# A new step list for a one-core transformer layer, 64x64 tiles for the W1 products, and MLP weights transposed on the host

## What is computed

```python
# attention part: 4 heads of 64 with fast weights W0, W1, W2; 4 chunks of 128 tokens
def step(carry, xi):
    W0, W1, W2, M0, M1, M2 = carry
    out = einsum(silu(qi @ W0.T) * (qi @ W2.T), W1)
    dhidden = einsum('bco,boh->bch', vi, W1)
    ...
    dw0 = dw0 + M0 * mm                      # and dw1, dw2
    dw0 = _newtonschulz5(dw0)                # five iterations: A = X X^T, B = bA + cAA, X = aX + BX
    return renorm(W0 + dw0, n0), ...
# beside it: windowed softmax attention with 2 heads of 128; both sums go through Wo
x = x + _layernorm(attention(_layernorm(x)))
# MLP
h = gelu(xn @ proj1.T + proj1_bias)          # proj1 (1024, 256)
out = h @ proj2.T + proj2_bias               # proj2 (256, 1024)
x = x + _layernorm(out)
```

## Time and profile before

| | |
|---|---|
| median of 3 runs | 419.19 us |
| profiled execution | 418.44 us |
| its span, first to last instruction | 416.7 us |
| mean granted TensorE clock | 0.994 |
| PE busy | 387.9 us (93%) |
| PEld busy | 310.6 us (75%) |
| DVE busy | 273.9 us (66%) |
| ACT busy | 225.7 us (54%) |
| POOL busy | 195.3 us (47%) |
| HBM traffic | 24 GB/s |

### The profile page before, as it was taken

One profiled execution on the slowest core, in us unless ns is written; L12 is line 12 of the kernel. 1 busy time (PEld: TensorE's weight loads), 2 busy tenths in 40 slices (PEclk: granted clock), 3 DMA queues, 4 the chain that ended last, 5 costly groups with the idle time before them and its releaser, 6 DMA issues.

```text
span 416.7 us, 15706 instructions
## 1 busy us (share of the span) xinstructions
PE 387.9 (93%) x6574; PEld 310.6 (75%) x6574; DVE 273.9 (66%) x720; ACT 225.7 (54%) x444; POOL 195.3 (47%) x273
## 2 busy tenths in 40 slices
PE   5998997999999999988999999997989999998994
PEld 5477856887668887877667888776788757886883
DVE  3359998788245869897545883888657582587113
ACT  1599654556852378635994632562445674444510
POOL 4366673557551534675250592643235070367114
PEclk9899999999999999999999999999999999999999
DMA  6830100000000000022000000000300000010001
GB/s 155 294 95 5 49 2 2 5 4 5 2 2 4 13 3 2 2 77 70 3 2 6 5 0 2 2 2 4 104 5 3 5 2 2 1 52 0 2 1 50
DMA packets 12293, 10.83 MB, mean 26 GB/s; under 512 B 4160, under 2 KB 11712, under 8 KB 12224
## 3 DMA queue, kind: packets, MB, share of 16 engines
q1 hardware_dynamic: 12224, 9.83, 7.7%
HBM read 7.73 MB, written 2.10 MB: 24 GB/s over the span
## 4 chain that ended last, share of the span: by engine, by line
PE 64%; DVE 10%; issue 5%; POOL 5%; ACT 1%; POOLq 0%; DVEq 0%; ACTq 0%
PE pair L782 14%; PE pair L791 9%; PE pair L684 6%; PE pair L672 6%; PE pair L697 5%; PE pair L661 4%; PE pair L750 3%; PE pair L566 3%; POOL fro L1389 2%; PE pair L717 2%; PE pair L538 2%; PE pair L623 1%; PE pair L609 1%; POOL u_n L1389 1%; PE pair L547 1%
## 5 line engine op out<-in xcount | busy, mean ns | idle before, releaser
L782 PE MATMUL pair<-xn2T,p1T 128*128 128x512 f32 (+1 forms) x160 | 58.1, 511 | 0.6 <-ACT xn2T L815 0.6
L791 PE MATMUL pair<-p2T,h 128*128 128x256 f32 x256 | 56.7, 381 | 0.0
L1394 POOL TENSOR_SCALAR var<-mv 128x1 f32<-128x1 f32 (+1 forms) x52 | 12.3, 236 | 90.5 <-DVE mv L1358 56.5
L791 PEld LDWEIGHTS pair<-p2T,h 128*128 128x128 f32 x256 | 48.2, 190 | 6.4
L782 PEld LDWEIGHTS pair<-xn2T,p1T 128*128 128x128 f32 x160 | 29.4, 190 | 19.5 <-issue 17.5
L1059 DVE SCALAR_TENSOR_TENSOR A<-pair,eye 128x512 f32<-128x512 f32 x45 | 28.6, 683 | 15.4 <-PE pair L672 15.2
L822 ACT ACT_TABLE_LOAD x28 | 35.9, 1283 | 2.1 <-PEq L1535 1.7
L1059 DVE SCALAR_TENSOR_TENSOR B<-pair,eye 128x512 f32<-128x512 f32 x45 | 28.9, 683 | 10.5 <-PE pair L684 10.5
L1035 ACT ACTIVATE h<-pair,b 128x512 f32<-128x512 f32 (+1 forms) x40 | 23.4, 602 | 19.8 <-PE pair L782 19.6
L1389 POOL TENSOR_TENSOR rstd<-var,neg_half 128x1 f32<-128x1 f32 (+1 forms) x52 | 31.7, 609 | 4.3
L684 PEld LDWEIGHTS pair<-A 64*64 64x64 f32 x1440 | 25.0, 134 | 9.9 <-issue 9.4
(11 more groups left out here) (166 smaller groups left out, 838.4 us busy)
## 6 DMA issues: line engine op xcount, KB each, us to landing
x_in<-in_L_attn_x_dram SPq DMA_DIRECT2D x4, 512.0 KB, 4.6
h<-in_L_ffn_proj_dram SPq DMA_DIRECT2D x2, 1024.0 KB, 6.8
x<-in_L_attn_x_dram SPq DMA_DIRECT2D x4, 512.0 KB, 4.8
out_dram<-rows_a SPq DMA_DIRECT2D x16, 128.0 KB, 1.7
wqkv<-in_L_attn_Wqkv_dram SPq DMA_DIRECT2D x1, 768.0 KB, 5.6
wo<-in_L_attn_Wo_dram SPq DMA_DIRECT2D x1, 256.0 KB, 7.9
X<-in_L_attn_w_dram SPq DMA_DIRECT2D x6, 32.0 KB, 2.2
b<-in_L_ffn_proj_bias_dram SPq DMA_DIRECT2D x1, 128.0 KB, 3.9
```

The lines of the kernel that those rows point to most:

```text
L782: mm_ = pe.matmul(ps[:, at], p1T[:, k, n * P:(n + 1) * P], xn2T[:, k, at], start=(k == 0), stop=(k == KC - 1))
L791: mm_ = pe.matmul(ps[:, 0:DIM], h[:, n, b * P:(b + 1) * P], p2T[:, n, :], start=(n == 0), stop=(n == HC - 1))
```

## The change

Four things change.

1. The list `ORDER` is another one: the same steps, but for MT, in another order. The MLP and attention steps stand at other points of the Newton-Schulz rows.
2. MT is gone, on PE and on ACT. The host hands in proj1 and proj2 transposed, and SP loads them straight into `p1T` and `p2T`. F1 and F2 wait for these loads.
3. DH and OUT use four 64x64 tiles (`QUADS`), with the 128 tokens in two halves: 32 matmuls in place of 16.
4. The waits for `consts` ahead of the products are gone from PE.

```diff
-    w_sq=1, w_ss=1, w_norm=1, mt_ps=8, mlp_T=8,
+    w_sq=1, w_ss=1, w_norm=1,
...
-    NQ.0.2 WX.0.0 WX.0.1 QK.0.3 WX.0.2 SI.0.3 VV.0.3 MS.0 NQ.0.3 SM.0 NR.0.1 NR.0.2 NR.0.3 TR.0.0 TR.0.1 TR.0.2 MT.0.0
+    QK.0.3 VV.0.3 NQ.0.2 SI.0.3 NQ.0.3 NR.0.1 NR.0.2 TR.0.0 TR.0.1 TR.0.2 TR.0.3 NR.0.3 SM.0 WX.0.0 WX.0.1 WX.0.2
...
-            sp.dma_start(p1_raw[:, :, :], proj1.rearrange("(n p) e -> p n e", p=P)).then_inc(ld_p1, 16)
-            sp.dma_start(p2_raw[:, :, :], proj2.rearrange("(k p) n -> p k n", p=P)).then_inc(ld_p2, 16)
+            sp.dma_start(p1T[:, :, :], proj1T.rearrange("(k p) n -> p k n", p=P)).then_inc(ld_p1, 16)
+            sp.dma_start(p2T[:, :, :], proj2T.rearrange("(n p) e -> p n e", p=P)).then_inc(ld_p2, 16)
...
             def DH(bank, c):
-
-                pe.wait_ge(consts, 1)
                 take_pair(bank[0], "dh", c, 1)
...
-                        for r in range(2):
-                            mm_ = pe.matmul(BANK[bank[r]][:, at:at + HD], tttT[64 * r:64 * r + 64, 2, j, b, :],
+                        for r, half_ in QUADS:
+                            tokens = slice(64 * half_, 64 * half_ + 64)
+                            mm_ = pe.matmul(BANK[bank[r]][tokens, at:at + HD], tttT[64 * r:64 * r + 64, 2, j, b, tokens],
                                             W[64 * r:64 * r + 64, G_W1, 2 * b + (j ^ (b & 1)), :], start=True, stop=True)
...
-                        for col in range(2):
-                            mm_ = pe.matmul(BANK[bank[col]][:, at:at + HD], gT[64 * col:64 * col + 64, bp, 2 * (col ^ y_) + j, :],
-                                            W1T[64 * col:64 * col + 64, b, j, :], start=True, stop=True)
+                        for r, half_ in QUADS:
+                            tokens = slice(64 * half_, 64 * half_ + 64)
+                            mm_ = pe.matmul(BANK[bank[r]][tokens, at:at + HD], gT[64 * r:64 * r + 64, bp, 2 * (r ^ y_) + j, tokens],
+                                            W1T[64 * r:64 * r + 64, b, j, :], start=True, stop=True)
...
                 if c == 0 and n == 0:
-                    pe.wait_ge(*S["mlp_T"](0, 8))
+                    pe.wait_ge(ld_p1, 16)
...
+                if c == 0 and b == 0:
+                    pe.wait_ge(ld_p2, 16)
...
-        a = np.ascontiguousarray(inputs[name])
+        a = np.ascontiguousarray(inputs[name].T if name in _TRANSPOSED else inputs[name])
```

More of the change, by code:

```diff
@@ L142 @@
[L142 to L146, removed]
@@ L371, in layer_kernel @@
         rstd4 = sb("rstd4", BATCH)
-        p1_raw, p2_raw = share(h, 0, HC, DIM), share(h, HC * DIM, KC, HID)
         gba_t, one_t, dxh, gms = (share(h, n * 1024, 2, 8, HD) for n in range(4))
@@ L758, in NT @@
                 mm_.then_inc(S["nt_ps"].sem, 1)
-            def MT(bank, c, n):
-                ps = take(bank[0], "mlp_T", c, n + 1)
-                pe.wait_ge(ld_p1 if n < 4 else ld_p2, 16)
-                for q in range(4):
-                    if n < 4:
-                        blk = p1_raw[:, 4 * (n % 2) + q, (n // 2) * P:(n // 2 + 1) * P]
-                    else:
-                        col = (2 * (n - 4) + q // 2) * P
-                        blk = p2_raw[:, q % 2, col:col + P]
-                    mm_ = pe.transpose(ps[:, q * P:(q + 1) * P], blk, ident[:, :])
-                mm_.then_inc(S["mt_ps"].sem, 1)
             def F1(bank, c, n, part=None):
```

106 lines of the change are left out of this document (51 added, 55 removed).

## The result

The changed kernel took **406.40 us** (median of 4 runs, 404.49 to 407.96) against 418.57 us of the kernel before (4 runs, 415.91 to 420.74). The ratio is 0.971, with a 95% interval of 0.9635 to 0.9785. The profiled execution took 407.33 us; its span was 405.5 us and its granted clock 0.988. In this document a few executions that ran longer than the others of their version (1283.95 us once with the old tiles, 418.02 with all but the list, 423.74 with MT gone only) are left out of the ratios, though not of the medians.

What follows compares the result with a forecast made beforehand. PE was taken to bound most of the kernel, with some stops for other engines' chains and late instructions. Sum: 418.4 - 3.5 - 6.6 - 2.0 + 1.4 + 2.0 - 1.5 = 408.2 us, range 403.3 to 414.5.

Steps and rivals of the forecast that it cites:

- the prediction's signs: Trace signs listed beforehand; DVE or ACT stalls within Newton-Schulz rows, 5 us or more, would show it wrong.
- MT gone, and the start: Chunk 0: 5.4 us of PE work goes, 4.0 kept, +1.4 stall; first NA at 63 to 64, not 67.78.
- The clock rival: PE idle around 28 to 33 us puts the next stretch at 1.2 GHz: +1.7, 409.9; 0.3 of the forecast's share.
- the walk: Following the new list through chunk 0 with the old durations; first NA at 63 to 64 us.
- DH and OUT (6.6): Seven DH and OUT steps in 64x64 tiles: 1.05 us against 2.00 each, 6.6 us saved; bounds 0 and 6.6.
- The DW rival: 64x64 tiles in DH and OUT cost as much as DW's records, all 6.6 us gone: 414.8; chance 0.05.
- The consts waits: Removing PE's waits for consts ahead of the products gains 0; bounds 0 and 0.5 us.
- Supply: Late instruction blocks in runs of 64x64 products cost 8.5 us before, 6.5 after: gain 2.0, bounds 0 and 3.
- the model: Every 256-instruction block on PE, counted from 194, costs what its products lack of 3.15 us.
- short blocks: Blocks of 256 PE instructions, nearly all 64x64 products, with less work than the 3.15 us a block needs to come.
- Boundary of chunk 1 to 2: Less PE work fills the 13.0 us momentum chain before the last X: +2.0 of stall, bounds 0 and +3.
- Last chunk: Two F2 steps of chunk 2 fill PE's waits at the layer norm: -1.5 us, bounds 0 and -2.

Runs made afterwards that it cites:

- the old tiles: Changed kernel with DH and OUT put back to their old form (16 matmuls, 128 columns of weights): 412.38 us.
- all but the list: Changed kernel with the step order of the kernel before, less the MT steps: 413.11 us.
- MT gone only: Kernel before with only the MT steps removed and the weights transposed by the host: 420.06 us.
- the run with 11 dummies: Changed kernel with its 24 dummy transposes at the start replaced by 2 transposes and 11 dummy matmuls of 512 columns: 408.28 us.
- the shift of 64: Changed kernel with 64 more PE instructions (waits for a raised semaphore) behind the first dummy transposes: 414.91 us.
- new tiles only: Kernel before with only DH and OUT in 64x64 tiles: 422.37 us.
- five steps moved: Changed kernel with five MLP and attention steps moved 2 to 5 places in the list, same program length: 403.99 us.
- 16 instructions: Changed kernel with 16 more PE instructions (waits for a raised semaphore) behind the first dummy transposes: 406.99 us.
- the two versions of the kernel before: Kernel before with only MT removed, 420.06 us, and kernel before with only DH and OUT in 64x64 tiles, 422.37 us.
- the two last versions: Changed kernel with 2 dummy matmuls at the start plus five moved steps, 402.56 us; the same with chunk 0's waits filled, 402.89 us.

## Why the prediction was right or wrong

**What bounds the kernel.** Right. Less work on PE was less time, as far as it was not replaced by a wait; the mean share of PE stayed at 93%. One wait of 1.33 us for DVE stands ahead of the first NA of chunk 1 (at 177.95). By the prediction's signs such a wait speaks against it, but it took the place of one of 0.96 us ahead of the X before, and is far from the 5 us that it names.

**MT gone, and the start (booked +1.4 of stall, 4.0 kept).** Wrong in the profiled execution: the first NA came at 67.04 and not at 63 to 64, so 0.7 was kept. The step that failed is that the start was walked through with the durations of before, and with them its clock. PE's wait ahead of the first transposes was 2.20 us and the clock was low from about 10 to 17 us. The clock rival had the mechanism, but placed it at 28 us and priced it at 1.7; there, with the new list, a low clock cost 0 to 0.5 us. The profiles with the new list whose clock stayed full at the start put the first X of the last matrix at 63.1 to 63.9 (but for the run with 11 dummies, whose start is late), so the walk was right for the full clock. Without dummy matmuls an execution gets one or the other, so this term was in part a matter of chance. "MT gone only" showed that this part alone keeps nothing.

**DH and OUT (6.6).** Right: 1.09 to 1.20 us in the chain against 1.79 to 2.00, so 0.85 in place of 0.95 each, 6.0 in all. Undoing it cost 6.0 too, but with other gaps at block ends. The DW rival falls. The estimate by the floor of the Trainium skill ("TensorE: Matmul & The Clock Gate", section "Wait — 56ns, not 53.3ns?"), 1.6 us a step, does not agree with these rows either; 64 records take 1.09 us with the last end, 17 ns each.

**The consts waits (0, bounds 0 and 0.5).** Wrong: with them back the kernel takes 4.2 us more. The bounds looked at the wait itself. It has a price of its own that they held too small, 1.6 us of busy time in these rows, and an instruction also costs by shifting the program (2.7 us). The second part was in the forecast's count of blocks; the first was in no term.

**Supply (2.0).** Right in mechanism, and shown by the shift of 64 and by the packets of the instruction queue. The size is rough: the gaps at block ends fell by 1.2 us, from 6.4 to 5.2. Over larger changes of place they grew by 5.2 where the model gave +3.7 (64 instructions) and by 7.5 for +4 (new tiles only), and fell by 2.6 for -4.3 (five steps moved) and by nothing that can be told for -1.2 (16 instructions). The block is not a fixed 3.15 us. In the changed kernel the short blocks with a gap took 3.53 to 3.91 us each, and the gap at one place differs by up to 0.6 us between traces (1.29 and 0.70 at 3521). The prediction also has 126 records at 1.84 us, 0.0146 each, where its own row gives 0.0164, so 2.07. The rule "mostly hidden" of the Trainium skill ("Runtime: NRT & Kernel Launch", section "Instruction fetch mechanics") does not hold in these rows of 64x64 tiles: 5.2 us of open gaps in this trace, 13.9 in that with only the tiles changed.

**Boundary of chunk 1 to 2 (+2.0).** Wrong: PE waits 1.10 us ahead of the last X, before 1.30, and not about 3. The chain from the momentum to that X is 276.26 - 264.16 = 12.1 us against 13.0. DVE also starts on the momentum 0.2 us ahead of PE's last row of DW (264.16 and 264.35), where it had started 0.8 us behind it (271.07 and 270.25). The two make 1.9 us. The step that failed took the chain as fixed and the filler as the only thing that moved. I had named MU ahead of DW in the list as the bound at 0, and that end was the right one.

**Last chunk (-1.5).** Right, a little too much. Of the three waits of 0.57, 0.45 and 0.56 one of 0.33 is left, 1.2 us less, and the two F2 steps cover the layer norm.

**What no term held.** The busy time of NA, NB and NX fell by 3.8 us (81.4 to 77.6) with the same records. The runs place it: 79.2 us with the waits put back, 80.4 with the old list, and 81.5 and 81.9 in the two versions of the kernel before. So the waits have about 1.6 of it and the new list most of the rest. Why a list with more other steps between these rows runs them in less busy time is open.

**Altogether.** The start was 3.3 us worse than booked, the boundary 2.2 better, tiles, supply and last chunk together 1.6 worse, and the Newton-Schulz rows 3.8 better. As measured, the terms are 0.7 for chunk 0, 4.2 for the five later tile steps, 1.2 for supply, 0.2 for the boundary and 1.2 for the last chunk, 7.5 us; with the 3.8 they are 11.3 of the 11.2 us between the profiled spans. The forecast came out 1.8 above the median because these cancelled. Its range held in part because it was built from the ends of each term, but the closeness of 408.2 was luck.

## What to carry to other kernels

Look at where the gaps without a releaser stand in the program. If they sit at one remainder of 256 and end just behind a packet of the instruction queue, as here, then a stretch of very short matmuls outruns its instructions, and an edit that adds or removes instructions ahead of it can move the time by 1% or 2%: 64 instructions cost 2%, and two edits that took work away from PE made this kernel slower. Before an edit is judged by its time, shift the program by some tens of instructions and see how far the time moves by that alone. Work that fills a wait on another engine's chain is free until it is taken away, and then the wait and the clock behind it are the price.

## What the runs showed of the hardware

- A shift of 64 instructions cost 8.5 us (414.91 against 406.40) with the same work in the same order; in its profile 5.2 us of this are gaps at block ends, and 1.5 us the instructions themselves, 46 ns each (2.92 us of idle time for 64) of which about half lies in a wait that was there already.
- In fourteen traces all 93 gaps of 0.3 us and more at block ends that no engine releases end 1.20 to 1.59 us behind the landing of a packet of the instruction queue. In the changed kernel the blocks that such a gap follows took 3.53 to 3.91 us each.
- Where no other step cuts in, 96 records in 64x64 tiles take 1.56 to 1.57 us in the chain and 64 take 1.09, 16 to 17 ns each; 32 records with 128 columns of weights take 2.00.
- PE at 1.2 GHz: from 12 to 15 us the clock was granted 0.50 after a wait of 2.20 us ahead of the first real transposes, but 0.52 and 0.56 after ones of 0.79 and 1.02 too, and 1.00 after ones of 1.19, 1.54 and 1.80. From 31.8 to 35.4 us it was granted 0.50 after waits of 2.83 and 1.30 us. The length of the wait alone does not decide it, and this gives no limit.
- Mean clock and time are loosely tied here: 0.987 to 0.999 in runs of the two last versions, with medians 0.3 us apart.
